# Moving indirect scatters of routed rows, and the experts' second result scatter, on GpSimd's queue

## The reference, cut to what matters

```
x = x + tanh(g_xattn) * attention(layernorm(x), ctx, ctx, masks)      # 16 heads of 8, 64 keys
h = layernorm(x)
probs = softmax(h @ router_w + router_b)                              # 8 experts
top 2 of probs, normed to sum 1 -> combine
moe = sum_e combine[e] * (gelu((h @ w1[e] + b1[e]) * gate[e]) @ w2[e] + b2[e])
y = moe + sigmoid(shared_weight) * shared_expert(h)
out = x + tanh(g_ffn) * (layernorm(y) * ln_g + ln_b)
```

## Time and profile before

| | |
|---|---|
| median of 3 runs | 815.27 us (813.66 to 815.3) |
| the profiled execution's own time | 814.22 us |
| its span, first to last instruction | 812.4 us |
| PE busy | 703.1 us, 87% |
| DVE busy | 619.3 us, 76% |
| ACT busy | 526.3 us, 65% |
| POOL busy | 274.6 us, 34% |
| mean granted TensorE clock | 0.95 |

### The profile page before, as it was taken

One profiled execution on the slowest core, in us unless ns is written; L12 is line 12 of the kernel. 1 busy time (PEld: TensorE's weight loads), 2 busy tenths in 40 slices (PEclk: granted clock), 3 DMA queues, 4 the chain that ended last, 5 costly groups with the idle time before them and its releaser, 6 DMA issues. The chain is left out here.

```text
span 812.4 us, 25014 instructions
## 1 busy us (share of the span) xinstructions
PE 703.1 (87%) x8074; PEld 546.8 (67%) x8075; DVE 619.3 (76%) x2328; ACT 526.3 (65%) x1117; POOL 274.6 (34%) x293
## 2 busy tenths in 40 slices
PE   2799999999999999999953799999999998967930
PEld 1466666666666666666631599999999997945620
DVE  5788988888888888888764577766666664629998
ACT  2678877878778787777520565666555664528873
POOL 5000033222333223233345146655555554520000
PEclk9999999999999999999955999999999999989975
DMA  4111121222321232311113822222222222244552
GB/s 126 40 41 48 54 81 44 70 65 76 84 81 51 61 88 73 83 42 38 38 47 132 207 67 78 75 78 68 74 69 75 73 70 62 68 114 135 171 145 87
DMA packets 74961, 64.59 MB, mean 80 GB/s; under 512 B 8320, under 2 KB 62848, under 8 KB 74624
## 3 DMA queue, kind: packets, MB, share of 16 engines
q1 hardware_dynamic: 53360, 32.96, 16.1%
q0 software_dynamic: 8448, 17.45, 6.6%
q10 hardware_dynamic: 13072, 13.12, 5.1%
HBM read 36.22 MB, written 23.09 MB: 73 GB/s over the span
## 5 line engine op out<-in xcount | busy, mean ns | idle before, releaser
L181 POOL DMA_INDIRECT expert_lists<-xn,slots x128 | 124.5, 973 | 311.9 <-PE pair L421 194.6
L1257 ACT ACTIVATE hT<-pair,b1g_c,gate_c 128x256 f32<-128x256 f32 x272 | 138.4, 562 | 101.5 <-PE pair L79 94.8
L1382 POOL DMA_INDIRECT expert_results<-y,dest x136 | 138.9, 1022 | 130.6 <-DVE y L1359 81.3
L1196 PE MATMUL pair<-w,hT 128*128 x1088 | 134.7, 277 | 0.0
L1196 PEld LDWEIGHTS pair<-w,hT 128*128 128x128 f32 x1088 | 127.0, 192 | 2.1 <-issue 0.5
L898 ACT ACTIVATE PT<-pair 128x512 f32<-128x512 f32 x128 | 75.5, 591 | 45.0 <-PE pair L434 45.0
L77 PE MATMUL pair<-rT,w_now 128*128 128x256 f32 x276 | 83.8, 303 | 4.6 <-ACT hT L1257 3.8
L577 DVE TENSOR_REDUCE mx<-pair 128x16 f32<-128x1024 f32 x64 | 78.2, 1223 | 10.0 <-PE pair L404 8.5
L1330 DVE CAST w_now<-w 128x1024 fp32r x71 | 52.7, 742 | 36.3 <-issue 36.3
L79 PE MATMUL pair<-rT,w_now 128*128 128x256 f32 x276 | 78.5, 284 | 0.0
L78 PE MATMUL pair<-rT,w_now 128*128 128x256 f32 x276 | 78.4, 284 | 0.0
(11 more groups left out here) (182 smaller groups left out, 1422.8 us busy)
## 6 DMA issues: line engine op xcount, KB each, us to landing
rows<-expert_lists SPq DMA_DIRECT2D x70, 130.0 KB
yin<-expert_results SPq DMA_DIRECT2D x16, 512.0 KB, 5.3
x_all<-in_x SPq DMA_DIRECT2D x16, 256.0 KB, 4.5
cT<-in_ctx_T SPq DMA_DIRECT2D x16, 256.0 KB
pad_k<-in_mask_BxS_ik SPq DMA_DIRECT2D x16, 256.0 KB
xn2T<-x2T ACTq DMA_DIRECT2D x16, 256.0 KB
w<-in_w ACTq DMA_DIRECT2D x4, 1024.0 KB, 15.2
out<-res ACTq DMA_DIRECT2D x7, 512.0 KB, 4.6
```

What stands on the lines that cost most here:

```text
L181: po.indirect_dma_start(lists[:, :], bass.IndirectOffsetOnAxis(ap=m.slots[:, par, t, k:k + 1], axis=0), m.xn2[:, par, t, :], None).then_in ...
L1196: last = pe.matmul(y_ps[par][:, h * D:(h + 1) * D], hT[:, par, c, h * P:(h + 1) * P], w2[:, bass.ds(e, 1), c, :].rearrange("p a d -> p (a ...
L1257: ac.activation(hT[:, par, c, :], h_ps[par][c // 2][:, (c % 2) * SL:(c % 2 + 1) * SL], ACT.Gelu, bias=b1g_c[:, c, bass.ds(e, 1)], scale=ga ...
L1382: po.indirect_dma_start(results[:, :], bass.IndirectOffsetOnAxis(ap=dest[:, par, h, :], axis=0), y[:, par, h, :], None).then_inc(sent[par] ...
```

## The change

In attention, quads 0 to 12 get two sends in each of four tile steps (u = 2, 3 of one quad, u = 0, 1 of the next): the first of a step after `masked` of tile n, the second after `turned` of tile n-1. No send waits for `subbed` any more. For quads 13 and 14 the pairs wait for stages of a later quad's routing. In the experts, the second half of `y` of step t-1 is sent in body t, behind a separate wait for `h_done` of step t+1, and before the first half of step t.

```diff
-            def scatter(n, q, par, first, count=3):
+            def scatter(n, q, first):
                 need(po, rb_step, q, per=RB_STEPS, total=NQ)
-                need(po, subbed, n - 1)
-                scatter_rows(po, lists, m, q, (first,))
-                need(po, masked, n)
-                scatter_rows(po, lists, m, q, (first + 1,))
-                if count == 3:
+                if q < NQ - 3:
+                    need(po, masked, n)
+                    scatter_rows(po, lists, m, q, (first,))
                     need(po, turned, n - 1, per=2)
-                    scatter_rows(po, lists, m, q, (first + 2,))
+                    scatter_rows(po, lists, m, q, (first + 1,))
+                else:
+                    if q == NQ - 3:
+                        need(po, *((lg_done, q + 1), (lgT_done, q + 1), (pref_done, q + 1),
+                                   (xn2_ready, q + 2, QT))[first // 2], total=NQ)
+                    else:
+                        need(po, (x2T_done, lg_done, lgT_done, pref_done)[first // 2], q + 1, total=NQ)
+                    scatter_rows(po, lists, m, q, (first, first + 1))
...
-                    if u == 2 and exists(q - 3, NQ - 1):
-                        scatter(n, q - 3, 1 - par, 0)
-                    if u == 3 and exists(q - 3, NQ - 1):
-                        scatter(n, q - 3, 1 - par, 3)
-                    if u == 0 and exists(q - 4, NQ - 1):
-                        scatter(n, q - 4, par, 6, 2)
+                    if u >= 2 and exists(q - 3, NQ - 1):
+                        scatter(n, q - 3, 2 * u - 4)
+                    if u < 2 and exists(q - 4, NQ - 1):
+                        scatter(n, q - 4, 2 * u + 4)
...
+            def send(par, h):
+                po.indirect_dma_start(results[:, :], bass.IndirectOffsetOnAxis(ap=dest[:, par, h, :], axis=0),
+                                      y[:, par, h, :], None).then_inc(sent[par], 16)
+
             def body(t, par, i):
+                if not isinstance(t, int) or t >= 1:
+                    wait_apart(po, h_done, (t + 1) * HB + HB)
+                    send(1 - par, 1)
                 po.wait_ge(dest_ready, t + 1)
                 wait_apart(po, y_ready, t + 1)
-                for h in range(2):
-                    po.indirect_dma_start(results[:, :], bass.IndirectOffsetOnAxis(ap=dest[:, par, h, :], axis=0),
-                                          y[:, par, h, :], None).then_inc(sent[par], 16)
+                send(par, 0)
             iterations(po, body)
+            send(1, 1)
```

## The result

The changed kernel takes 822.18 us (median of 5 runs, 821.3 to 823.55) against 814.58 for the kernel before (5 runs on the same chip, among them the runs of the table ahead of the prediction): ratio 1.0086, 95% interval 1.0073 to 1.0099, 0.9% slower. It was compared again on two other chips, beside the kernel before each time: 1.0072 (1.005 to 1.0094) where the kernel before takes 787.84, and 1.010 (1.0075 to 1.0125) where it takes 815.68. A fourth chip, used for parts of the change only, takes 842.23 for the kernel before.

What follows compares the result with a forecast made beforehand. POOL was nowhere the bound by its own work; the question was whom its sends hold up, with attention's beat the scores-to-subtraction chain. 0 + 1.3 + 0 on 815.27 gave 816.6 us, its own range 815.3 to 819, overall 804 to 821.

Steps and rivals of the forecast that it cites:

- Part 1: Attention, quads 0 to 12: same eight sends a quad, no added POOL work; taken as 0 us.
- bound of 3.9: Attention: upper bound, 0.30 us more in u = 0 of each of 13 quads.
- 0.30 of u = 0: Attention: step 16, with a send behind `masked`, takes 6.10 us against 5.80 in step 12 without a scatter.
- u = 2's cost, nothing: Attention: the new send behind `masked` in u = 1 costs nothing, as in u = 2, since L434 comes late.
- Rival 3: Experts' loop: later second send starts inside DVE's cast, ends 0.42 later; 10.9 us more, 827.5; chance 0.12.
- Part 2: Drain, quads 13 and 14: POOL's waiting pairs become last, next block at 441.2 instead of 439.92; +1.3 us.
- the five microseconds at L975: Drain: ACT's 5.78 us idle before L975, awaiting L502's answer; claimed recoverable without any gain.
- Part 3: Experts: second send's added wait for `h_done` moves it 0.1 to 0.3 us every second step; taken as 0.
- rival 1: Experts' loop: fewer late PE answers, 0.50 us less an iteration, 13.0 in all, 803.6; chance 0.34.
- That wait is met before it is reached: Experts' loop: `h_done` comes by 563.6, while `y` is ready only at 564.66, so the added wait holds nothing.
- Rival 2: Attention: the pause was due to the send behind `subbed`; 7 to 9 us less, 807.6; chance 0.06.

Runs made afterwards that it cites:

- carried: Changed kernel with two calls exchanged, so the send itself carries the wait for `masked`; second chip 836.43 us, ratio 0.9924 to the kernel before.
- no_masked: Changed kernel, first send of each step in quads 0 to 12 behind the previous step's `subbed`, not `masked`; third chip 790.06 us, ratio 1.003 to before.

## Why the prediction was wrong

**Part 1 failed, and with it the number.** I forecast 1.3 us more than before and measured 7.6. I took 0 for attention, between -9 and +3.9; it lost 6.1 us on the first chip, 6.6 on the fourth. The step that failed is the sentence "The sends behind `masked` of u = 0, 2 and 3 stay where they are, so their cost stays". They moved by 0.5 us: in the kernel before the send behind `masked` has no other wait; in the changed one it also calls for `rb_step`, and `masked` goes to an instruction of its own. I counted POOL's sends and which semaphore each stands behind, and not the wait instructions between. The terms are: u = 3 gained 0.39 and u = 0 0.05, because a send at 0.75 lets L434 through; u = 2 lost 0.45 and u = 1, where the send behind `masked` is new and starts at 0.75 too, lost 0.50. The bound of 3.9 was too narrow for a second reason: it took the 0.30 of u = 0 as the most that a send can cost, though the pause itself is longer, and looked at L434 alone. In u = 1 and 2 it is the values L450 that the pause falls into.

"u = 2's cost, nothing" was right for the send at 0.24, and nearly so for the new place in u = 1: carried shows 6.02 in both, where attention as before has 5.94 in u = 1. The observation under it, that what matters is where PE is when POOL ends its descriptors, is what the experiments confirmed. I had the mechanism and applied it to the wrong places. Why PE is held at that time the traces do not show, only when.

**Rival 3 was the right thing at the wrong place.** I looked for a send that starts beside a cast in the experts, where nothing moved. It happened in attention: L582 went from 0.18 to 0.43. The rule of "SBUF — State Buffer", section "Who interferes with whom", in the Trainium skill, that only VectorE and GpSimd share ports, agrees with that cast on all four chips. PE does not fit it: 30 + 2 values with the send at 0.75, 32 in one piece with it at 0.24, on the first, second and fourth chip; on the third nothing in the steps contradicts the rule.

**Part 2 was right, its size in part by luck.** Predicted 1.3, measured 1.2 on the first chip, 1.5 on the second and 3.0 on the fourth. Of these, 0.2, 1.0 and 2.1 came from in front of quad 13's slots, so the drain's edit itself cost 1.0, 0.4 and 0.9. "the five microseconds at L975 can be won back without any gain": 0.77 idle there, the last L181 behind L466 of quad 15, POOL last, 2.34 from its end to the next block where I had 2.54.

**Part 3 was right for the loop of the first chip** (1.27 apart, 7.3 an iteration) and so was the doubt about rival 1 there. "That wait is met before it is reached" failed at the loop's end, where it gained 1.9, and in 9 of the loop's 34 steps on the second chip, where a gain of rival 1's kind came in: shorter late answers, not fewer, by the wait that I called met. Rival 2 fell: carried has no send behind `subbed` in attention, and its u = 0 still takes 6.12; and no_masked has one in every step, with u = 0 at 5.81. That attention takes 8.9 us less with the sends away from `masked`, where I had written 7 to 9 for this rival, is a coincidence of size.

## What to carry to other kernels

Before moving an instruction that another engine's short work depends on, write down its start within the step to a tenth of a microsecond before and after, its wait instructions included; here a second semaphore on it moved it by 0.5 us and made 6 us of 815. Ask of each send whom it meets 0.8 to 1.3 us after its start, and put it where the answer is nobody: behind the end of a step's chain, not at its head. Here that was worth 8.9 us in attention on the fourth chip; on the third, where PE is not held, the kernel with its sends placed so did not beat the one before. A small stall that a reordering takes away in a drain is worth only the distance to the next engine that is late.

## What the runs showed of the hardware that I had not expected

- The same program on four chips takes 787.84, 814.58, 815.68 and 842.23 us. What differs most is how long PE is held around GpSimd's sends: in attention u = 1 takes 6.43 to 6.46 with the send at 0.75 on three chips, and 5.93 on the third; in the experts' loop steps of 3.64 and 3.22 on the third, 3.04 and 4.28 on the first and fourth, up to 6.7 on the second. Why chips differ in this was not tested.
- Of two semaphores called for ahead of a send, the one called for last gets the instruction of its own. The send starts 0.75 us after L577, which waits for the same semaphore, and 0.24 after it when the send carries the wait itself; exchanging two calls moves it by 0.5.
- A cast of DVE of 128 x 32 that starts inside a send's descriptors ends with them: 0.43 in place of 0.18. DVE's maxima L577, which run under the same send, keep their 1.22 to 1.23.
